# Key-value sums of the first pass as split products, with the pass's buffers laid out anew

## The chip, the cores and the metric

The kernel runs on one core of a Trainium2 chip. The metric is the device time of one launch in microseconds (us). Three runs of the kernel before took 457.25, 457.77 and 458.14 us, so the median is 457.77 us. Lower is better.

## The reference, cut to what matters

Four sequences of 2048 tokens with 256 features pass through a linear-attention block, a feed-forward block, a small iterative attention block that touches the first 16 tokens of every sequence, and the feed-forward block again. The change lies in the linear attention alone:

```python
x = _layernorm(x)                       # (4, 2048, 256)
q = elu(x @ Wq + bq) + 1                # 16 heads of 16 features
k = elu(x @ Wk + bk) + 1
v = x @ Wv + bv
kv = jnp.einsum('bkhd,bkhm->bhdm', k, v)      # sums over all tokens of a sequence
out = jnp.einsum('bqhd,bhdm->bqhm', q, kv) / max(q . sum(k), 1e-6)
```

The kernel doesn't form `v`. Since `v` is linear in the normalised tokens, it sums the 256 x 256 matrix G = kᵀ x over the tokens of a sequence, and multiplies G by Wv once per sequence. The last of the 256 columns of the normalised tokens is replaced by ones, which gives the sum of the keys for the normaliser. All of it is fp32. A product of fp32 accuracy is either one fp32 matmul, or several matmuls of type fp32r on a "high" part (the value rounded to fp32r) and a "low" part (what is left of it).

## The kernel before, in words

A *group* is 512 tokens: 4 tiles (`T = 4`) of 128 tokens. There are 16 groups (`NG`), 4 (`G`) to each of 4 sequences (`B`); n numbers the groups and g is n's place in its sequence. Pass 1 goes once over all groups, computing queries (kept in `q_all`) and G; pass 2 then goes over them again for everything else. Each engine has its own in-order program, the same loop `pass1(b, last)` on each of them, and they meet by semaphores only. The first sequence is unrolled, sequences 1 and 2 run in a hardware loop, the last is unrolled.

One group n of pass 1, engine by engine, in the order of each queue:

- TensorE (PE): `k_product(n)` is 24 fp32r matmuls of 256 columns into `PB` (L1212 to L1214); `q_product(n)` is 12 fp32r matmuls of 512 columns into `PA` (L1226 to L1228); `t1(n+1)` transposes the next group's normalised tokens into `PT` (L1168); `g_product(n)` is 8 fp32 matmuls of 256 columns into `PG` (L1236), each recorded as two. It waits for `k_done`.
- ScalarE (ACT): `ln1(n+1)` normalises the next group, 4 instructions (L535), after the statistics of group n+1 are in (`rstd1`) and after `g_product(n-1)`, which read the buffer of `xn` that is written; `exp_k` (L570) after `k_product(n)`; `exp_q` (L576) after `q_product(n)`; the high part `xt_hi` of the next group's transposes (L546, two).
- VectorE (DVE): the keys `k_tok` (L821) after `exp_k`; the layer-norm statistics of group n+2 (L740, L743); the low part `xt_lo` of the next group's transposes (L768, two) for which `k_product(n+1)` waits; the queries (L830).
- GpSimd (POOL): four small instructions that turn the statistics of a group into its scale and shift (L416 to L422; L418 is a power), and then `add_bo`, which adds a bias row to the tokens of the group before, 1024 elements a lane (L429).
- SyncE only loads tokens and weights.

At the first group of sequences 1 to 3, G of the sequence before is finished: DVE copies it to `g_sb` (L837), PE transposes it (L1244), ACT copies that (L583), PE multiplies by Wv (L1253, between the halves of `q_product`), and DVE masks the result into `kv_all` (L844, L848). Between the first and the second sequence DVE also prepares late weights: L784, L785, L787 and L855. All of them but L785 read two operands from SBUF.

`xn` has two buffers, `k_tok` one, and `exp_k` and `exp_q` share one.

Of the kernel before, what the change touches and what calls it, by code (L numbers as in the profile page):

```python
# [18 lines left out]
T = 4  # L19
# [25 lines left out]
def hybrid_kernel(nc, x_in, Wq, bq, Wk, bk, Wv, bv, Wo, bo, qw, qb, kw, vw, vb, ow, ob,  # L45
# [18 lines left out]
    with ExitStack() as ctx:  # L64
# [43 lines left out]
        SCR = 9 * 1024 + 8  # L108
        scratch = sb("scratch", [P, SCR])
        used = [0]  # L110

        def part(n):
            a = scratch[:, used[0]:used[0] + n]
            used[0] += n
            assert used[0] <= SCR
            return a

        xn = [part(T * D).rearrange("p (t d) -> p t d", t=T) for _ in range(2)]
# [4 lines left out]
        setup_start = used[0]  # L123
        wq_raw = part(C * D).rearrange("p (c n) -> p c n", c=C)
        wk_raw = part(C * D).rearrange("p (c n) -> p c n", c=C)
        bq_rows, bk_rows = part(D), part(D)
        minus_last, ident_less, to_last = [part(P) for _ in range(3)]
        used[0] = setup_start + 2 * C * GT
        wv, wo_raw = [part(C * D).rearrange("p (c n) -> p c n", c=C) for _ in range(2)]
        wv_last, bv_rows, bo_rows = [part(D) for _ in range(3)]  # L130
        g_sb = part(C * D).rearrange("p (c n) -> p c n", c=C)
        token_of = part(B * P)
        used[0] = 0
        o_tok = part(T * D).rearrange("p (k n) -> p k n", k=T * C)
        x2t = part(C * GT).rearrange("p (c n) -> p c n", c=C)
        h2, h2s, h3 = part(GT), part(GT), part(GT)
        y3 = part(T * D // 2).rearrange("p (t d) -> p t d", d=D)
        w1c = part(C * F).rearrange("p (c f) -> p c f", c=C)
# [4 lines left out]
        squares = o_tok.rearrange("p k n -> p (k n)").rearrange("p (c n) -> p c n", c=C)  # L143


        with ExitStack() as pass1_memory:
            def sb1(name, shape):
                return pass1_memory.enter_context(nc.sbuf_tensor(name, shape, F32R))

            wq_hi, wq_lo = sb1("wq_hi", [P, C, D]), sb1("wq_lo", [P, C, D])  # L150
            wk_hi, wk_lo = sb1("wk_hi", [P, C, D]), sb1("wk_lo", [P, C, D])
            xt_hi, xt_lo = sb1("xt_hi", [P, C, GT]), sb1("xt_lo", [P, C, GT])
# [8 lines left out]
        raw4 = [b_weights[:, 0, i, :].rearrange("p (c n) -> p c n", c=C) for i in range(4)]  # L161
        folded_all = b_weights[:, 1, :, :].rearrange("p i n -> p (i n)")
# [34 lines left out]
        after_raw = carve(b_weights[:, 0, :, :].rearrange("p i n -> p (i n)"))  # L197
# [16 lines left out]
        def one_batch_columns(wide):  # L214
# [25 lines left out]
        q_mm, q_exp, q_done = sem("q_mm"), sem("q_exp"), sem("q_done")  # L240
        g_mm, g_copied, gt_mm, gt_copied, kv_mm, kv_done = [
# [18 lines left out]
        (c_wts, c_vecs, c_xs, c_out, c_blk, c_bd, c_bd_sb, c_brow, c_brow_sb, c_fold, c_fold_sb, c_stat, c_rstd, c_z, c_zt, c_zt_sb,  # L260
         c_qkv, c_lin, c_k, c_vi, c_ss, c_rs, c_lt, c_q1, c_kn, c_knt, c_knm, c_vsel, c_vm, c_logit, c_lg, c_pr, c_pt, c_p1,
         c_inv, c_pv, c_o, c_ot, c_ot_sb, c_ql, c_dsum, c_diff, c_flag, c_proj, c_hid, c_relu, c_sq, c_ffn, c_added, c_final, c_zero,
         c_pool) = [sem(f"c_{n}") for n in (
             "wts", "vecs", "xs", "out", "blk", "bd", "bd_sb", "brow", "brow_sb", "fold", "fold_sb", "stat", "rstd", "z", "zt", "zt_sb",
             "qkv", "lin", "k", "vi", "ss", "rs", "lt", "q1", "kn", "knt", "knm", "vsel", "vm", "logit", "lg", "pr", "pt", "p1",
             "inv", "pv", "o", "ot", "ot_sb", "ql", "dsum", "diff", "flag", "proj", "hid", "relu", "sq", "ffn", "added", "final", "zero",
             "pool")]
# [41 lines left out]
        def _(sp):  # L309
# [69 lines left out]
            sp.wait_ge(c_final, 1)  # L379
# [10 lines left out]
        def _(pool):  # L390
# [45 lines left out]

            ln1(0)
            pool.wait_ge(norm1_dve, 2)
            ln1(1)
            pool.wait_ge(w2_loaded, 16 * 8)  # L440
            add_bo(0)
            with pool.Fori(2, NG) as n:
                ln1(n)
                add_bo(n - 1)
            add_bo(NG - 1)
# [84 lines left out]
        def _(act):  # L530
# [31 lines left out]
            def pass1(b, last):  # L562
                for g in range(G):
                    n = b * G + g
                    if not (last and g == G - 1):
                        ln1(n + 1, g + 1)

# [5 lines left out]
                    act.wait_ge(k_done, n + 1)  # L573

# [10 lines left out]
            act.wait_ge(setup_dve, 1)  # L585
            pass1(0, False)
# [140 lines left out]
        def _(dve):  # L727
# [84 lines left out]
            def pass1(b, last):  # L812
                for g in range(G):
# [122 lines left out]
            def step(g, b):  # L936
# [63 lines left out]
                if runs(r):  # L1000
# [4 lines left out]
                    if r == NG - 1:  # L1005
                        nc.vector.tensor_copy(dsum[0:SP, 7:8], x_s_out[:, 0:1]).then_inc(c_final, 1)
# [42 lines left out]
            def chain(i, slot):  # L1049
# [21 lines left out]
                elif at == (6, 1):  # L1071
                    dve.wait_ge(c_qkv, 1)
                    dve.wait_ge(c_brow_sb, 2)
                    nc.vector.tensor_tensor(kc.rearrange("p (c n) -> p c n", c=C), PG[0:SP, 0, D:2 * D].rearrange("p (c n) -> p c n", c=C),
                                            bias_k.rearrange("p (o n) -> p o n", o=1).to_broadcast([SP, C, P]), ALU.add).then_inc(c_k, 1)
                    nc.vector.tensor_tensor(lin, PG[0:SP, 0, 0:D], bias_q, ALU.add).then_inc(c_lin, 1)
                    nc.vector.tensor_tensor(vi, PG[0:SP, 1, 0:D], bias_v, ALU.add).then_inc(c_vi, 1)
                    dve.wait_ge(c_k, 1)
                    square_sums(kc, 0)
                elif at == (7, 1):  # L1080
                    dve.wait_ge(c_rs, 1)
                    link(nc.vector.tensor_tensor(heads(kc), heads(kc), over_feats(inv_std[0]), ALU.mult))
                    nc.vector.tensor_tensor(heads(kc), heads(kc), over_heads(l_w), ALU.mult).then_inc(c_kn, 1)
                    dve.wait_ge(c_vsel, 1)
# [3 lines left out]
                elif at == (7, 3):  # L1088
                    dve.wait_ge(c_knt, 1)
# [511 lines left out]
```

## Time and profile before

| | us |
|---|---|
| median of three runs | 457.77 |
| the profiled execution | 457.29 |
| its span, first to last instruction | 455.5 |
| TensorE busy | 425.2 (93%) |
| VectorE busy | 293.2 (64%) |
| ScalarE busy | 183.8 (40%) |
| GpSimd busy | 203.5 (45%) |
| granted TensorE clock, mean | 0.993 |

The time of the profiled execution is 1.8 us more than its span; it is 0.5 us below the median. Pass 1 takes the first 180 us of the span. Busy shares are means over the whole kernel, so they say which engine to look at, and the timelines of single engines within one group say what sets the pace there. In a timeline a row gives start, duration, engine, line, operation, and what it writes and reads; the duration of a TensorE row includes its pipeline, so the pace of matmuls is read from the chain of work, where a row's time is what it adds. Small GpSimd instructions are best read from start to start.

### The profile page before, as it was taken

Reading aid. Unit: us, or ns where it says so; the run is one execution under the profiler, and the core shown is the slowest. Engines: PE = TensorE matmul, PEld = TensorE weight load, DVE = VectorE, ACT = ScalarE, POOL = GpSimd, SP = SyncE. Lnnn points to the kernel's source line nnn. Section 1 sums busy time; section 2 is a strip of 40 time slices with the busy share of each in tenths; the row PEclk is TensorE's granted clock in tenths of the full one; section 3 lists DMA queues with packets and bytes.
Section 4 is the critical chain, followed back from the end, with each engine's and each line's share of the span. In section 5 each row is a group of like instructions: output and inputs, shape, how many; then the busy total and the mean of one; then the engine's idle time right before and its main releaser. Section 6 shows DMA issues by size and latency. Waiting matters only on the chain.

```text
span 455.5 us, 7618 instructions
## 1 busy us (share of the span) xinstructions
PE 425.2 (93%) x2570; PEld 354.7 (78%) x2570; DVE 293.2 (64%) x651; ACT 183.8 (40%) x321; POOL 203.5 (45%) x334
## 2 busy tenths in 40 slices
PE   7799989999999999688979999999999999999971
PEld 4689979998898999676858876878777787787851
DVE  4565575455556543459637697878858777887843
ACT  2464545555455541224134532333243323424440
POOL 3344442433334350036144367566527527635562
PEclk9999999999999999999999999999999999999997
DMA  8512111111100003100110111011010111011102
GB/s 260 179 48 78 63 47 46 48 46 46 46 0 1 0 2 89 8 2 3 51 46 4 50 49 35 15 48 47 4 47 1 50 48 35 16 49 47 48 32 71
DMA packets 22776, 20.58 MB, mean 45 GB/s; under 512 B 3255, under 2 KB 22717, under 8 KB 22717
## 3 DMA queue, kind: packets, MB, share of 16 engines
q1 hardware_dynamic: 22156, 19.32, 13.5%
q8 instruction: 30, 0.49, 0.4%
q10 hardware_dynamic: 560, 0.52, 0.4%
q14 instruction: 30, 0.24, 0.2%
HBM read 11.32 MB, written 8.45 MB: 43 GB/s over the span
## 4 chain that ended last, share of the span: by engine, by line
PE 82%; DVE 7%; ACT 5%; issue 2%; POOL 2%; DMA 1%; POOLq 0%; ACTq 0%; DVEq 0%
PE PG L1236 11%; PE PB L1356 6%; PE PT L1395 6%; PE PA L1356 5%; PE PB L1377 5%; PE PA L1425 4%; PE PA L1431 3%; PE PA L1426 3%; PE PA L1226 3%; PE PA L1227 3%; PE PA L1228 3%; PE PB L1214 3%; PE PB L1212 3%; PE PB L1213 3%; PE PT L1435 3%; PE PA L1367 3%
## 5 line engine op out<-in xcount | busy, mean ns | idle before, releaser
L454 POOL TENSOR_TENSOR ln_a<-ln_bn 128x4 f32<-128x4 f32 x32 | 6.5, 205 | 132.0 <-DVE ln_bn L934 132.0
L1236 PE MATMUL PG<-scratch 128*128 128x256 f32 x256 | 58.0, 379 | 1.3 <-DVE scratch L821 1.3
L821 DVE SCALAR_TENSOR_TENSOR scratch<-scratch,PB 128x1024 f32<-128x1024 f32 x16 | 19.5, 1221 | 60.3 <-ACT scratch L570 60.3
L1236 PEld LDWEIGHTS PG<-scratch 128*128 128x128 f32 x256 | 47.4, 190 | 7.4 <-issue 1.5
L535 ACT ACTIVATE scratch<-x_all,ln_shift,ln_rstd 128x255 f32 (+1 forms) x60 | 31.1, 589 | 36.7 <-PE PG L1236 30.2
L934 DVE BATCH_NORM_STATS2 ln_bn<-x_all 128x6 f32<-128x256 f32 x128 | 44.9, 413 | 0.9
L416 POOL TENSOR_SCALAR ln_rstd<-ln_mv 128x4 f32<-128x4 f32 x16 | 3.7, 228 | 91.3 <-DVE ln_mv L743 88.4
L1212 PE MATMUL PB<-wk_hi,xt_hi 128*128 128x256 f32 x128 | 39.0, 305 | 0.4 <-DVE xt_lo L768 0.4
L429 POOL TENSOR_TENSOR x_all<-x_all,scratch 128x1024 f32 (+1 forms) x16 | 38.2, 2388 | 0.6 <-ACT scratch L535 0.5
L429 POOL TENSOR_TENSOR x_all<-x_all,ob_rows 128x1024 f32<-128x1024 f32 x16 | 37.8, 2360 | 0.0
L695 ACT ACTIVATE scratch<-PA,ln_rsq 128x256 f32<-128x256 f32 x32 | 13.4, 471 | 59.3 <-PE PA L1356 35.4
L1425 PE MATMUL PA<-wo_hi,o_hi 128*128 128x256 f32 x128 | 33.5, 295 | 3.1 <-ACT o_hi L702 2.7
L1214 PE MATMUL PB<-wk_hi,xt_lo 128*128 128x256 f32 x128 | 36.2, 282 | 0.0
L1213 PE MATMUL PB<-wk_lo,xt_hi 128*128 128x256 f32 x128 | 36.1, 282 | 0.0
L463 POOL TENSOR_TENSOR ln_rsq<-ln_a,minus_ones 128x4 f32<-128x4 f32 x32 | 32.5, 1015 | 2.5
L1356 PE MATMUL PA<-ws,scratch 128*128 128x256 f32 x128 | 30.4, 380 | 2.7 <-ACT scratch L688 2.7
L990 DVE TENSOR_TENSOR x_all<-PA,x_all 128x1024 f32<-128x1024 f32 x16 | 19.6, 1225 | 20.6 <-PE PA L1431 20.6
L977 DVE TENSOR_TENSOR o_lo<-PB,o_hi 128x512 fp32r<-128x512 f32 x32 | 20.6, 684 | 18.6 <-ACT o_hi L702 18.5
L1426 PE MATMUL PA<-wo_lo,o_hi 128*128 128x256 f32 x128 | 31.9, 282 | 0.0
L1356 PE MATMUL PB<-ws,scratch 128*128 128x256 f32 x128 | 31.1, 386 | 0.0
L1395 PE MATMUL PT<-scratch 128*128 128x512 f32 x64 | 30.9, 605 | 0.0
L576 ACT ACTIVATE scratch<-PA,minus_one 128x1024 f32<-128x1024 f32 x16 | 17.8, 1115 | 30.2 <-PE PA L1228 28.9
(239 smaller groups left out, 1039.0 us busy)
## 6 DMA issues: line engine op xcount, KB each, us to landing
out_dram<-x_all SPq DMA_DIRECT2D x16, 512.0 KB, 3.1
x_all<-n_L_attn_a_inputs_q_dram SPq DMA_DIRECT2D x15, 512.0 KB, 3.6
x_all<-n_L_attn_a_inputs_q_dram ACTq DMA_DIRECT2D x2, 128.0 KB, 2.8
x_all<-n_L_attn_a_inputs_q_dram SPq DMA_DIRECT2D x2, 128.0 KB, 2.6
scratch<-in_L_attn_a_Wk_dram SPq DMA_DIRECT2D x1, 256.0 KB, 4.6
scratch<-in_L_attn_a_Wq_dram ACTq DMA_DIRECT2D x1, 256.0 KB, 5.0
scratch<-in_L_attn_a_Wv_dram SPq DMA_DIRECT2D x1, 256.0 KB, 6.8
scratch<-in_L_attn_a_Wo_dram SPq DMA_DIRECT2D x1, 256.0 KB, 6.2
```

The source lines that it names most:

```text
L429: nc.gpsimd.tensor_tensor(x_group(n), x_group(n), rows_[:, :].rearrange("p (o d) -> p o d", o=1).to_broadcast([P, T, D]), ALU.add).then_in ...
L463: nc.gpsimd.tensor_tensor(ln_rsq[:, slot, :], a, minus_ones[:, :], ALU.pow).then_inc(done, 1)
L535: nc.scalar.activation(dst[:, t:t + 1, 0:width], x_tile(n, t)[:, :, 0:width], ACT.Identity, scale=ln_rstd[:, slot, t:t + 1], bias=ln_shift ...
L934: nc.vector.bn_stats(ln_bn[:, slot, t:t + 1, :], x_tile(n, t)).then_inc(bn, 1)
L1212: mm(dst, hi, wk_hi[:, c, :], start=(c == 0), stop=False)
L1213: mm(dst, hi, wk_lo[:, c, :], start=False, stop=False)
L1214: last = mm(dst, lo, wk_hi[:, c, :], start=False, stop=(c == C - 1))
L1236: last = mm(PG[:, c, 0:D], k_tok[:, t, c * P:(c + 1) * P], xn[g % 2][:, t, :], start=(g == 0 and t == 0), stop=(g == G - 1 and t == T - 1))
L1356: last = mm(four(pair)[:, t, :], h[:, t * P:(t + 1) * P], ws2[:, :], start=True, stop=True)
L1395: last = mm(PT[:, 0, :], w1c[:, c, :], x2t[:, c, :], start=(c == 0), stop=(c == C - 1))
L1425: mm(four(PA)[:, t, :], hi, wo_hi[:, c, :], start=(c == 0), stop=False)
L1426: mm(four(PA)[:, t, :], hi, wo_lo[:, c, :], start=False, stop=False)
```

## The change

`g_product(n)` becomes two sets of fp32r matmuls. Keys are split into `k_hi` and `k_lo`, normalised tokens into the halves of `xn_pair`. The first set multiplies `k_hi` by both halves at once (8 matmuls of 512 columns, which fill a bank of `PG` with two sums), the second `k_lo` by the high half (8 of 256 columns). The high parts are copies by ACT (`x_high`, and the copy after `k_done`), `k_lo` is a subtraction by DVE ahead of `t1`, the low half of `xn_pair` a subtraction by POOL (`x_low`) behind `add_bo`. `ln1` on ACT now waits for `x_low` instead of `g_product`. The two sums of `PG` are added once a sequence by one more DVE instruction in `copy_g`.

`k_hi` and `k_lo` use the memory of `o_hi` and `o_lo`, which are idle in pass 1. The weights of set-up, of pass 1 and of pass 2 move to other places in SBUF, and the halves of `b_weights` swap. Eighteen single-use semaphores of the iterative attention become three counters (`c_once`, `c_made`, `c_taken`), with the same waits at the same places. Pass 2 issues the same instructions.

```diff
@@ POOL
+            def x_low(n, g):
+
+                ge_apart(pool, "pool", hi_done, 2 * n + 1)
+                nc.gpsimd.tensor_tensor(xn_pair[:, :, 1, :], xn[g % 2], xn_pair[:, :, 0, :].bitcast(F32), ALU.subtract).then_inc(x_lo, 1)
+
             ln1(0)
             pool.wait_ge(norm1_dve, 2)
             ln1(1)
+            x_low(0, 0)
             pool.wait_ge(w2_loaded, 16 * 8)
             add_bo(0)
-            with pool.Fori(2, NG) as n:
+            for n in range(2, G):
                 ln1(n)
                 add_bo(n - 1)
+                x_low(n - 1, n - 1)
...
@@ ACT
             def ln1(n, g):
-                ge_apart(act, "act", g_mm, n - 1)
+                ge_apart(act, "act", x_lo, n - 1)
                 normalise(xn[g % 2], n, 0, n, rstd1, norm1, D - 1)
+
+            def x_high(n, g):
+
+                ge_apart(act, "act", norm1, T * (n + 1))
+                ge_apart(act, "act", g_mm, n)
+                nc.scalar.activation(xn_pair[:, :, 0, :], xn[g % 2], ACT.Copy).then_inc(hi_done, 1)
...
                     if not (last and g == G - 1):
                         ln1(n + 1, g + 1)
+                    x_high(n, g)
 
                     act.wait_ge(k_mm, n + 1)
...
                     act.wait_ge(k_done, n + 1)
+                    nc.scalar.activation(k_hi, k_tok, ACT.Copy).then_inc(hi_done, 1)
 
                     ge_apart(act, "act", q_mm, C * (n + 1))
...
@@ DVE
                     if g == 0 and later_batch:
                         batch_kv(b - 1)
+                    dve.wait_ge(hi_done, 2 * n + 2)
+                    nc.vector.tensor_tensor(k_lo, k_tok, k_hi.bitcast(F32), ALU.subtract).then_inc(k_lo_done, 1)
                     if not (last and g == G - 1):
                         t1(n + 1, g + 1)
...
                 nc.vector.tensor_copy(g_sb[:, :, :], PG[:, :, 0:D]).then_inc(g_copied, 1)
+                dve.wait_ge(g_copied, 2 * b + 1)
+                nc.vector.tensor_tensor(g_sb[:, :, :], PG[:, :, D:2 * D], g_sb[:, :, :], ALU.add).then_inc(g_copied, 1)
@@ PE
-                pe.wait_ge(k_done, n + 1)
+                pe.wait_ge(hi_done, 2 * n + 2)
+                pe.wait_ge(x_lo, n + 1)
                 for t in range(T):
                     for c in range(C):
-                        last = mm(PG[:, c, 0:D], k_tok[:, t, c * P:(c + 1) * P], xn[g % 2][:, t, :],
-                                  start=(g == 0 and t == 0), stop=(g == G - 1 and t == T - 1))
+                        mm(PG[:, c, :], k_hi[:, t, c * P:(c + 1) * P], xn_pair[:, t, :, :].rearrange("p h d -> p (h d)"),
+                           start=(g == 0 and t == 0), stop=False, skip_group_check=True)
+                pe.wait_ge(k_lo_done, n + 1)
+                for t in range(T):
+                    for c in range(C):
+                        last = mm(PG[:, c, 0:D], k_lo[:, t, c * P:(c + 1) * P], xn_pair[:, t, 0, :],
+                                  start=False, stop=(g == G - 1 and t == T - 1), skip_group_check=True)
                 last.then_inc(g_mm, 1)
```

## Rows read from the trace of the kernel before

**Rows 1.** Page, part 4: shares of the chain of work that ended last.

```profile
PE 82%; DVE 7%; ACT 5%; issue 2%; POOL 2%; DMA 1%; POOLq 0%; ACTq 0%; DVEq 0%
```

**Rows 2.** Chain of work around group 9: start, time added, engine, tile, line.

```profile
112.95 0.12 PE PB L1214
113.07 0.23 PE PA L1226
...
115.82 0.87 PE PT L1168 x8
116.69 3.46 PE PG L1236 x16
```

**Rows 3.** Timeline of PE: the first matmul of `k_product` of groups 1, 3, 4, 5, 8, 9.

```profile
25.87 0.47 PE L1212 MATMUL PB<-wk_hi,xt_hi 128*128 128x256 f32 x1
...
45.76 0.47 PE L1212 MATMUL PB<-wk_hi,xt_hi 128*128 128x256 f32 x1
...
55.71 0.47 PE L1212 MATMUL PB<-wk_hi,xt_hi 128*128 128x256 f32 x1
...
68.57 0.47 PE L1212 MATMUL PB<-wk_hi,xt_hi 128*128 128x256 f32 x1
...
98.41 0.47 PE L1212 MATMUL PB<-wk_hi,xt_hi 128*128 128x256 f32 x1
...
109.85 0.47 PE L1212 MATMUL PB<-wk_hi,xt_hi 128*128 128x256 f32 x1
```

**Rows 4.** Timeline of DVE in group 9: keys, last of the statistics, low parts.

```profile
114.26 1.22 DVE L821 SCALAR_TENSOR_TENSOR scratch<-scratch,PB 128x1024 f32<-128x1024 f32 x1 [4.21 <-ACT scratch L570]
...
116.72 0.41 DVE L743 BATCH_NORM_AGGREGATE ln_mv<-ln_bn 128x2 f32<-128x6 f32 x4
117.58 1.29 DVE L768 TENSOR_TENSOR xt_lo<-PT,xt_hi 128x512 fp32r<-128x512 f32 x2 [0.45 <-ACT xt_hi L546]
```

**Rows 5.** Timeline of ACT in group 9.

```profile
110.55 2.08 ACT L535 ACTIVATE scratch<-x_all,ln_shift,ln_rstd 128x255 f32 x4 [2.47 <-PE PG L1236]
113.11 1.12 ACT L570 ACTIVATE scratch<-PB,minus_one 128x1024 f32<-128x1024 f32 x1 [0.48 <-PE PB L1214]
115.94 1.12 ACT L576 ACTIVATE scratch<-PA,minus_one 128x1024 f32<-128x1024 f32 x1 [1.72 <-PE PA L1228]
116.96 1.08 ACT L546 ACTIVATE xt_hi<-PT 128x512 fp32r<-128x512 f32 x2
```

**Rows 6.** Timeline of POOL in group 9: first statistics instruction, and `add_bo`.

```profile
117.40 0.23 POOL L416 TENSOR_SCALAR ln_rstd<-ln_mv 128x4 f32<-128x4 f32 x1 [7.02 <-DVE ln_mv L743]
...
119.47 2.39 POOL L429 TENSOR_TENSOR x_all<-x_all,scratch 128x1024 f32 x1
```

**Rows 7.** Timelines of ACT, DVE and POOL between the first two sequences.

```profile
53.79 0.64 ACT L588 ACTIVATE wo_hi<-scratch 128x512 fp32r<-128x512 f32 x1
...
55.86 2.42 DVE L784 TENSOR_TENSOR scratch<-scratch 128x512 f32<-128x512 f32 x1
...
58.92 0.68 DVE L855 TENSOR_TENSOR wo_lo<-scratch,wo_hi 128x512 fp32r<-128x512 f32 x1
...
55.32 2.41 POOL L429 TENSOR_TENSOR x_all<-x_all,scratch 128x1024 f32 x1
```

**Rows 8.** Groups of POOL by line, then DVE and POOL timelines where they overlap.

```profile
L461 POOL TENSOR_TENSOR ln_a<-ln_a,ln_d 128x4 f32<-128x4 f32 x32 | 6.7, 210 | 2.5
...
405.53 0.47 DVE L1138 SCALAR_TENSOR_TENSOR b_weights<-b_weights,q_all 64x256 f32<-64x256 f32 x1
...
405.61 0.45 POOL L461 TENSOR_TENSOR ln_a<-ln_a,ln_d 128x4 f32<-128x4 f32 x1
...
372.81 0.41 DVE L1095 TENSOR_TENSOR b_weights<-b_weights 64x256 f32<-64x256 f32 x1
...
372.71 1.02 POOL L463 TENSOR_TENSOR ln_rsq<-ln_a,minus_ones 128x4 f32<-128x4 f32 x1
```

**Rows 9.** Timeline of ACT in group 0: `exp_k`.

```profile
20.03 1.10 ACT L570 ACTIVATE scratch<-PB,minus_one 128x1024 f32<-128x1024 f32 x1
```

More of the change, by code:

```diff
@@ L105, in hybrid_kernel, with parts, take @@
         r_gap = sb("r_gap", [P, 4, T])
-        SCR = 9 * 1024 + 8
+        SCR = 4 * T * D
         scratch = sb("scratch", [P, SCR])
[L110 to L116, printed above, removed]
+        def parts(piece):
+            at = [0]
+            def take(n):
+                a = piece[:, at[0]:at[0] + n]
+                at[0] += n
+                assert at[0] <= piece.shape[1]
+                return a
+            return take
+        part = parts(scratch)
         xn = [part(T * D).rearrange("p (t d) -> p t d", t=T) for _ in range(2)]
@@ L122, in hybrid_kernel @@
         exp_q = exp_kq.rearrange("p (c n) -> p c n", c=C)
[L123 to L130, printed above, removed]
@@ L131, in hybrid_kernel @@
-        g_sb = part(C * D).rearrange("p (c n) -> p c n", c=C)
-        token_of = part(B * P)
-        used[0] = 0
+        k_hi, k_lo = [o[:, :, :].rearrange("p c n -> p (c n)").rearrange("p (t d) -> p t d", t=T) for o in (o_hi, o_lo)]
+        part = parts(scratch)
         o_tok = part(T * D).rearrange("p (k n) -> p k n", k=T * C)
         x2t = part(C * GT).rearrange("p (c n) -> p c n", c=C)
-        h2, h2s, h3 = part(GT), part(GT), part(GT)
+        h2, h3 = part(GT), part(GT)
         y3 = part(T * D // 2).rearrange("p (t d) -> p t d", d=D)
+        token_of = part(B * P)
@@ new lines, in hybrid_kernel, with sb1 @@
+        squares = o_tok.rearrange("p k n -> p (k n)").rearrange("p (c n) -> p c n", c=C)
+        with ExitStack() as pass1_memory:
+            def sb1(name, shape, dt=F32R, memory=pass1_memory):
+                return memory.enter_context(nc.sbuf_tensor(name, shape, dt))
+            with ExitStack() as setup_memory:
+                part = parts(sb1("setup", [P, T * 2 * D], F32, setup_memory))
+                wq_raw = part(C * D).rearrange("p (c n) -> p c n", c=C)
+                wk_raw = part(C * D).rearrange("p (c n) -> p c n", c=C)
+                bq_rows, bk_rows = part(D), part(D)
+                minus_last, ident_less, to_last = [part(P) for _ in range(3)]
+            xn_pair = sb1("xn_pair", [P, T, 2, D])
+            wq_hi, wq_lo = sb1("wq_hi", [P, C, D]), sb1("wq_lo", [P, C, D])
+            wk_hi, wk_lo = sb1("wk_hi", [P, C, D]), sb1("wk_lo", [P, C, D])
+            xt_hi, xt_lo = sb1("xt_hi", [P, C, GT]), sb1("xt_lo", [P, C, GT])
+            part = parts(sb1("wvo", [P, 9 * D], F32))
+            g_sb = part(C * D).rearrange("p (c n) -> p c n", c=C)
+            wv = part(C * D).rearrange("p (c n) -> p c n", c=C)
+            bo_rows = part(D)
+            wo_raw = part(C * D).rearrange("p (c n) -> p c n", c=C)
+            wv_last, bv_rows = part(D), part(D)
@@ L138, in hybrid_kernel @@
+        part = parts(sb("ffn_weights", [P, 5376 - GT])[:, :])
         w1c = part(C * F).rearrange("p (c f) -> p c f", c=C)
@@ L142, in hybrid_kernel @@
         ob_t = part(C * P).rearrange("p (c n) -> p c n", c=C)
[L143 to L152, printed above, removed]
+        h2s = sb("h2s", [P, GT])[:, :]
         b_weights = sb("b_weights", [P, 2, 4, C * D])
@@ L240, in hybrid_kernel @@
         q_mm, q_exp, q_done = sem("q_mm"), sem("q_exp"), sem("q_done")
+        hi_done, x_lo, k_lo_done = [sem(n) for n in ("hi_done", "x_lo", "k_lo_done")]
         g_mm, g_copied, gt_mm, gt_copied, kv_mm, kv_done = [
@@ L259, in hybrid_kernel @@
         c_link = sem("c_link")
[L260 to L267, printed above, removed]
+        c_wts, c_vecs, c_xs, c_out, c_blk, c_bd, c_brow, c_fold, c_fold_sb, c_stat = [sem(f"c_{n}") for n in (
+            "wts", "vecs", "xs", "out", "blk", "bd", "brow", "fold", "fold_sb", "stat")]
+        c_rstd, c_z, c_zt, c_zt_sb, c_lin, c_ss, c_rs, c_lt, c_q1, c_knm = [sem(f"c_{n}") for n in (
+            "rstd", "z", "zt", "zt_sb", "lin", "ss", "rs", "lt", "q1", "knm")]
+        c_vm, c_logit, c_lg, c_pr, c_pt, c_p1, c_inv, c_pv, c_o, c_ot = [sem(f"c_{n}") for n in (
+            "vm", "logit", "lg", "pr", "pt", "p1", "inv", "pv", "o", "ot")]
+        c_ot_sb, c_ql, c_zero, c_pool, c_once, c_made, c_taken = [sem(f"c_{n}") for n in (
+            "ot_sb", "ql", "zero", "pool", "once", "made", "taken")]
+        QKV, VSEL, KNT, DIFF, PROJ, HID, FFN = range(1, 8)
+        K, VI, KN, DSUM, FLAG, ADDED, FINAL = range(1, 8)
         waits_passed = {"sp": sem("sp_waits_passed"), "act": sem("act_waits_passed"),
@@ L439, in _ @@
             ln1(1)
+            x_low(0, 0)
             pool.wait_ge(w2_loaded, 16 * 8)
             add_bo(0)
-            with pool.Fori(2, NG) as n:
+            for n in range(2, G):
                 ln1(n)
                 add_bo(n - 1)
+                x_low(n - 1, n - 1)
+            with pool.Fori(1, B) as b:
+                for g in range(G):
+                    n = b * G + g
+                    ln1(n)
+                    add_bo(n - 1)
+                    x_low(n - 1, g + 1)
+            x_low(NG - 1, NG - 1)
             add_bo(NG - 1)
```

91 lines of the change are left out of this document (46 added, 45 removed).

## The prediction

> **What bounds the kernel now.** I read the chain of work first. It lies on TensorE for 82% [rows 1], and within pass 1 it is TensorE without a gap: in one group 24 steps of 0.12, 12 of 0.23, 0.87 for the transposes and 3.46 for the fp32 `g_product` [rows 2], in sum 9.97 us. The first matmuls of `k_product` confirm it: 9.95 us from group to group [rows 3]. Two kinds of group are longer: those that finish a sequence's G (11.44), and the one between the first and second sequence (12.86) [rows 3].
>
> Then I read the other engines' timelines within a group, because a shorter `g_product` only helps as far as they keep up. I count from e, the start of `exp_k` [rows 5]. DVE makes the keys from e+1.15 to e+2.37 and its statistics end at e+4.02 [rows 4]. POOL starts on them at e+4.29 and is done at e+6.35, where `add_bo` takes over until e+8.75 [rows 6]. ACT and DVE pass on the next transposes by e+5.8 [rows 4, 5]. So one circuit of `exp_k`, keys, transposes, next `k_product` has about 1 us of slack in 9.95, not more. The reader is to see that TensorE is the bound, with a circuit through the other three engines close behind.
>
> The third thing is how DVE and POOL disturb each other. L784, a DVE subtraction of 512 elements with two SBUF operands, took 2.42 us where L855 of the same size took 0.68; it began during `add_bo`, which ended at 57.73, and itself ended 0.55 us later [rows 7]. The reverse also shows: POOL's L461, 0.21 us in the mean of 32, took 0.45 when it began during DVE's L1138 (two SBUF operands), and ended 0.06 us after it [rows 8]. Instructions with an operand in PSUM run beside POOL unstretched: the low parts at 117.58 keep their 1.29 next to L416 [rows 4, 6]. The change adds one such instruction per group on each of the two engines.
>
> **The change part by part.**
>
> *TensorE.* Removed: 3.46 us a group. Added: 8 matmuls of 512 columns at 0.23 and 8 of 256 at 0.12 [rows 2], in sum 2.80. If nothing else bound, a group would take 9.3 us, and 16 groups would save 10.5.
>
> *ACT.* `x_high` and the `k_hi` copy, 1024 elements each from SBUF. The trace has none of that size; 1024 from PSUM take 1.12 [rows 5], and 512 from SBUF take 0.64 [rows 7]. Bounds are 1.12 and twice 0.64, 1.28. I take 1.16, near the lower, since one instruction has one overhead, and let the next instruction start after 1.06 (the two PSUM ones start 1.02 apart). Nothing hides them fully, since both stand ahead of something that is waited for: `x_high` ahead of `exp_k`, `k_hi` ahead of `exp_q` and of `g_product`.
>
> *Circuit A, through the keys.* From e: keys e+2.37, `k_hi` e+3.56, `exp_q` starts e+3.46, the two transposed high parts end by e+5.6. On DVE `k_lo` runs from e+4.0 to e+5.2 (twice L855's 0.68 less one overhead: 1.21, [rows 7]), and the low parts then end at e+6.4. `g_product` starts at e+3.6 and ends at e+6.5. `k_product(n+1)` starts about e+6.45, takes 2.9 and some 0.25 for its first matmul. So circuit A is 9.6 us, and the new TensorE time of 9.3 isn't reached: TensorE waits 0.3 us a group.
>
> *Circuit B, through the statistics.* `ln1(n+1)` on ACT stands ahead of `x_high(n)` and `exp_k(n)`, and it needs POOL's scale of group n+1, which comes from statistics made after the keys of n-1. From e of n-1: POOL done e+6.35, `ln1` until e+8.4, `x_high` until e+9.4, then `exp_k(n)`: 9.5 us, if POOL isn't held up. But `k_lo` holds DVE's two SBUF reads from e+4.0 to e+5.2, and L416 wants to begin at e+4.29. By rows 8 it ends about 0.06 after `k_lo`, 0.7 us later than now, with no more than 0.13 of it absorbed. Circuit B is then 10.1 us, longer than A, and longer than the 9.95 of now.
>
> *x_low.* 1024 elements on POOL, 2.39 by `add_bo` [rows 6], bounds 1.2 (DVE's L821 has as many elements, [rows 4]) to 3.5 (half as much again for the strided fp32r output, which no row shows). It starts at e+0.15 and ends at e+2.5, ahead of `g_product` at e+3.6 with 1 us to spare, and away from `k_lo`. In a normal group it costs nothing; at 3.5 it still ends in time.
>
> *Groups that finish a sequence.* There the statistics are made long before `k_lo`, which waits for L844, so the collision is nearly gone; POOL's power instruction (L463's kind) let DVE's L1095 run in its 0.41 [rows 8], so I don't let L418 block. TensorE saves its 0.65, and `ln1`'s delay carried over from the group before takes back 0.35: 11.15 for 11.44. The group after it takes 9.6. The addition in `copy_g`, 0.68 as L855 [rows 7], ends before `k_product` does: nothing.
>
> *Start.* `exp_k(0)` starts at 20.03 and `k_product(1)` at 25.87 [rows 3, 9]. Now `x_high(0)` stands ahead: `exp_k(0)` at 21.1, keys until 23.5, `k_hi` until 24.6. On POOL `x_low(0)` (21.2 to 23.6) pushes `add_bo(0)` to between 23.6 and 26.0. `k_lo(0)` is ready at 25.1, is blocked until 26.0 and ends at 27.2; the second low part ends at 28.4. `k_product(1)` starts at 28.45: +2.6. L416 follows `k_lo(0)`, POOL is done at 29.1, and `ln1(2)` and `x_high(1)` put `exp_k(1)` at 32.1. The next three groups are 10.1 each: +0.45. So `k_product(4)` starts at 58.75 and `exp_k(4)` at 62.4.
>
> *Between the first two sequences.* Before, L784 waited for `add_bo` [rows 7], and the rest fitted. Now POOL has `add_bo(4)` from 59.3 to 61.7 and, as soon as `x_high(4)` ends at 62.5, `x_low(4)`. L784 ends 0.55 after `add_bo(4)`, at 62.25; L785 follows; L787 is ready at 62.5, a draw with `x_low(4)`. If it loses, it waits until 64.95 and takes 0.47 (L1138's time, [rows 8]), and L855 ends at 66.1; if it wins, L855 loses the next draw and ends at about the same time. Before, L855 ended at 59.6, and `k_product` of the next group started 8.97 later [rows 3, 7]. Now TensorE saves 0.65 of that and the addition in `copy_g` puts 0.68 on it: 75.05. The group takes 16.3 for 12.86: +3.45.
>
> *Rest.* In the last group nothing covers the `k_hi` copy: `exp_k(15)` comes 3.2 after the start of `k_product(15)`, and 3.56 and 2.8 later `g_product` ends. That is 9.6, against 9.4 by the same count with keys at 2.37 and `g_product` at 3.46, or +0.2 (at least 0, as `g_product(15)` can't start sooner than TensorE is free; at most 0.9, all of the exposed copy). Behind it the added `copy_g` instruction is hidden: TensorE has the first products of pass 2 ahead of the transposes of G. Uncovered it would cost its 0.68. Pass 2 issues the same work; new places in SBUF and shared counters: 0, as no wait is added. Set-up: 0.
>
> Sum, new less old: start +2.6; groups 1 to 3 +0.45; between sequences +3.45; sequence 1 (9.6, 10.1, 10.1 against three of 9.95) -0.05; sequence 2 (11.15, 9.6, 10.1, 10.1) -0.35; sequence 3 (11.15, 9.6, 10.1) -0.5; last +0.2. That is +5.8 on the profiled 457.29: 463.1, taken as 463.0. The profiled execution lies 0.5 under the median of the three runs, inside the rounding of this sum.
>
> **The rivals.**
>
> *POOL isn't delayed by `k_lo`.* L461 is a single case, and L1138 has 64 lanes. Then circuit B is 9.5 and A sets the pace: 0.46 less in 7 groups, 0.3 in 2, 0.5 at the boundary: -4.3, so 458.7.
>
> *Faster: operations with an fp32r output stay off the shared resource.* Every stretched DVE row writes plain fp32, and L855, the one with fp32r output, met no POOL instruction [rows 7]. Its place is wherever `k_lo`, L855 and `x_low` meet the other engine, its price what the sum charges there: the 4.3 above, 1.0 at the start, 2.4 where L787 would not wait for `x_low(4)`. It decides once circuit A (9.6) is the longest in most groups. 463.0 - 7.7 = 455.3. Against it: the reads are as in L784.
>
> *`x_low` is dear.* At 3.5 us it lengthens the start and the blocked L787 by 1.1 each: 465.2; and if two of the late-weight instructions are blocked instead of one, 467.6.
>
> *The power instruction blocks too.* By the row it doesn't. The Trainium skill ("SBUF — State Buffer", section on the two separate sides) says that the pair of ports shared by DVE and GpSimd is locked for the whole instruction and the loser fully blocks, for a DVE operation with two SBUF inputs as well. It agrees with L784 and L461; for L1095, which ran in 0.41 inside a power instruction, the trace disagrees. As a mechanism here: `k_lo` is blocked by L418 in the two groups that finish a sequence and behind the boundary, 0.7 each: 465.1.
>
> **How the numbers follow.** Forecast 0.50 (own range 461 to 465.5); POOL not delayed 0.14; faster 0.12; dear `x_low` 0.14; power blocks 0.06; the rest mishaps on either side. A measurement can tell about 0.2%, 0.9 us. Slower by more: 0.50 + 0.14 + 0.06 and half of POOL not delayed, with some of the rest, 0.79; same 0.09; faster 0.12. The range is 458.0 to 467.0; it takes in all but the faster case and the far end.
>
> **What would show each step.** Starts of `k_product` 10.1 apart in most groups, 9.6 in one after each G: circuit B. L416 ending just after `k_lo`: the blocking. L787 or L855 near 2.7 us: the boundary. `k_product(1)` at 28.4: the start. `k_product` starts 9.6 apart throughout mean that POOL runs on; 9.3 that both circuits are mis-sized. The prediction is wrong above all if `k_lo` and L416 don't meet.

## The result, and the profile after

The changed kernel takes 466.12 us in the median (465.63 to 467.02), against 457.95 us for the kernel before measured beside it: a ratio of 1.018, with a 95% interval of 1.015 to 1.0205. It is 8.2 us slower. The forecast was 463.0 us, in a range of 458.0 to 467.0.

The profiled execution of the changed kernel took 466.44 us. First the page: its span, and the shares of the chain of work that ended last.

```profile
span 464.7 us, 7704 instructions
...
PE 57%; DVE 14%; ACT 13%; issue 7%; POOL 5%; DVEq 1%; DMA 1%; POOLq 1%; ACTq 0%
```

The chain was 82% TensorE before [rows 1]. Now a quarter of it lies on VectorE and ScalarE: TensorE has less to do in pass 1 and no longer sets the pace there. The first matmuls of `k_product`, the counterpart of [rows 3], for groups 1, 3, 4, 6, 7 and 8:

```profile
29.56 0.36 PE L1257 MATMUL PB<-wk_hi,xt_hi 128*128 128x256 f32 x1
...
49.03 0.36 PE L1257 MATMUL PB<-wk_hi,xt_hi 128*128 128x256 f32 x1
...
59.02 0.36 PE L1257 MATMUL PB<-wk_hi,xt_hi 128*128 128x256 f32 x1
...
87.41 0.34 PE L1257 MATMUL PB<-wk_hi,xt_hi 128*128 128x256 f32 x1
...
97.57 0.34 PE L1257 MATMUL PB<-wk_hi,xt_hi 128*128 128x256 f32 x1
...
107.72 0.33 PE L1257 MATMUL PB<-wk_hi,xt_hi 128*128 128x256 f32 x1
```

Normal groups are 10.15 us apart, where it was 9.95. The same starts for all groups, read from the timelines of both kernels, give the whole account of the 9.2 us between the spans:

| stretch | before | after | difference | forecast |
|---|---|---|---|---|
| until `k_product(1)` starts | 25.87 | 29.56 | +3.7 | +2.6 |
| groups 1 to 3 | 29.84 | 29.46 | -0.4 | +0.45 |
| group 4, between the first two sequences | 12.86 | 18.89 | +6.0 | +3.45 |
| rest of sequence 1 | 29.84 | 29.81 | 0.0 | -0.05 |
| sequence 2 | 41.28 | 41.39 | +0.1 | -0.35 |
| sequence 3 without its last group | 31.34 | 30.78 | -0.55 | -0.5 |
| last group, to the end of `g_product(15)` | 9.42 | 9.76 | +0.35 | +0.2 |
| pass 2 and end of the span | 275.05 | 275.05 | 0.0 | 0 |

So the loss is at two places, and the other fourteen groups together come out 0.5 us shorter. One normal group, on ScalarE, VectorE and GpSimd (the counterparts of [rows 4 to 6]; L609 is `exp_k`, L578 `x_high`, L868 `k_lo`, L458 `x_low`, L434 the first statistics instruction, L447 `add_bo`):

```profile
88.23 2.08 ACT L567 ACTIVATE scratch<-x_all,ln_shift,ln_rstd 128x255 f32 x4 [1.80 <-POOL ln_shift L440]
90.21 1.04 ACT L578 ACTIVATE xn_pair<-scratch 128x1024 fp32r<-128x1024 f32 x1
91.16 1.10 ACT L609 ACTIVATE scratch<-PB,minus_one 128x1024 f32<-128x1024 f32 x1
93.54 1.06 ACT L613 ACTIVATE o_hi<-scratch 128x1024 fp32r<-128x1024 f32 x1 [1.29 <-DVE scratch L862]
```

```profile
94.74 0.41 DVE L784 BATCH_NORM_AGGREGATE ln_mv<-ln_bn 128x2 f32<-128x6 f32 x4
95.07 1.19 DVE L868 TENSOR_TENSOR o_lo<-scratch,o_hi 128x1024 fp32r<-128x1024 f32 x1
96.18 1.28 DVE L809 TENSOR_TENSOR xt_lo<-PT,xt_hi 128x512 fp32r<-128x512 f32 x2
```

```profile
91.43 2.41 POOL L458 TENSOR_TENSOR xn_pair<-scratch,xn_pair 128x1024 fp32r<-128x1024 f32 x1 [1.01 <-ACT xn_pair L578]
95.43 0.92 POOL L434 TENSOR_SCALAR ln_rstd<-ln_mv 128x4 f32<-128x4 f32 x1 [1.59 <-DVE ln_mv L784]
```

L434 begins while `k_lo` runs and takes 0.92 instead of 0.23 [rows 6]; it ends 0.09 after `k_lo`. And ScalarE's three instructions follow each other without a gap behind a wait of 1.80 for GpSimd: `exp_k` is issued as soon as the queue lets it, not when `k_product` is done. That is circuit B of the forecast, as drawn.

### The profile page after: what moved, and what is told of

It reads as the page before. It is cut to its first block, busy times and chain, and to the rows that moved or that the text cites. A ratio compares the mean times of both kernels' runs of the same rounds, so it can differ in the third digit from the quotient of the medians.

```text
span 464.7 us, 7704 instructions
## 1 busy us (share of the span) xinstructions
PE 423.5 (91%) x2570; PEld 349.5 (75%) x2570; DVE 317.9 (68%) x671; ACT 213.2 (46%) x353; POOL 251.1 (54%) x350
## 4 chain that ended last, share of the span: by engine, by line
PE 57%; DVE 14%; ACT 13%; issue 7%; POOL 5%; DVEq 1%; DMA 1%; POOLq 1%; ACTq 0%
PE PB L1407 6%; PE PA L1407 5%; PE PT L1446 5%; PE PB L1428 5%; PE PA L1476 4%; ACT scratch L609 3%; PE PA L1482 3%; PE PA L1477 3%; ACT scratch L567 3%; PE PG L1282 3%; PE PT L1486 3%; PE PA L1418 2%; DVE ln_bn L781 2%; ACT o_hi L743 2%; ACT xn_pair L578 2%
## 5 line engine op out<-in xcount | busy, mean ns | idle before, releaser
L458 POOL TENSOR_TENSOR xn_pair<-scratch,xn_pair 128x1024 fp32r<-128x1024 f32 x16 | 38.4, 2400 | 25.2 <-ACT xn_pair L578 25.2
L1282 PE MATMUL PG<-xn_pair,o_hi 128*128 128x512 f32 x128 | 35.6, 422 | 8.0 <-ACT o_hi L613 7.1
L447 POOL TENSOR_TENSOR x_all<-x_all,wvo 128x1024 f32 (+1 forms) x16 | 38.5, 2404 | 0.1
L447 POOL TENSOR_TENSOR x_all<-x_all,ob_rows 128x1024 f32<-128x1024 f32 x16 | 37.7, 2358 | 0.0
L1257 PE MATMUL PB<-wk_hi,xt_hi 128*128 128x256 f32 x128 | 37.1, 290 | 0.4 <-DVE xt_lo L809 0.4
L1282 PEld LDWEIGHTS PG<-xn_pair,o_hi 128*128 128x128 f32 x128 | 23.9, 196 | 15.9 <-ACT o_hi L613 6.6
L434 POOL TENSOR_SCALAR ln_rstd<-ln_mv 128x4 f32<-128x4 f32 x16 | 11.9, 746 | 39.3 <-DVE ln_mv L784 36.2
L755 ACT ACTIVATE scratch<-PT,w1ob 128x512 f32<-128x512 f32 x16 | 11.0, 688 | 46.4 <-PE PT L1486 46.4
L1407 PE MATMUL PB<-ws,h2s 128*128 128x256 f32 x128 | 31.1, 386 | 0.0
```

Of the source, the lines that this page charges most:

```text
L447: nc.gpsimd.tensor_tensor(x_group(n), x_group(n), rows_[:, :].rearrange("p (o d) -> p o d", o=1).to_broadcast([P, T, D]), ALU.add).then_in ...
L458: nc.gpsimd.tensor_tensor(xn_pair[:, :, 1, :], xn[g % 2], xn_pair[:, :, 0, :].bitcast(F32), ALU.subtract).then_inc(x_lo, 1)
L1257: mm(dst, hi, wk_hi[:, c, :], start=(c == 0), stop=False)
L1282: mm(PG[:, c, :], k_hi[:, t, c * P:(c + 1) * P], xn_pair[:, t, :, :].rearrange("p h d -> p (h d)"), start=(g == 0 and t == 0), stop=False, ...
L1407: last = mm(four(pair)[:, t, :], h[:, t * P:(t + 1) * P], ws2[:, :], start=True, stop=True)
```

## The experiments

**Keeping TensorE busy in its long waits.** The two places that cost more than forecast have something in common that I had not charged. At the start and in group 4:

```profile
24.31 3.75 PE L1282 MATMUL PG<-xn_pair,o_hi 128*128 128x512 f32 x8 [3.25 <-ACT o_hi L613]
...
67.39 1.12 PE L1295 MATMUL PG<-ident,wvo 128*128 128x128 f32 x4 [5.26 <-DVE wvo L882]
...
69.16 0.63 PE L1273 MATMUL PA<-xt_hi,wq_lo 128*128 128x512 f32 x1
69.59 0.63 PE L1271 MATMUL PA<-xt_hi,wq_hi 128*128 128x512 f32 x1
```

Eight matmuls of 512 columns take 3.75 us behind a wait of 3.25, where a normal group has 2.13; and behind the wait of 5.26 in group 4 they follow 0.43 apart instead of 0.23. The mean granted clock of these stretches (the figure before DMA's share) fits:

```profile
core 0: us, PE busy (x) PEld busy (x) DVE busy (x) ACT busy (x) POOL busy (x), PEclk, DMA share, GB/s
...
24.00:36.00 12.00, 11.69 (x59) 10.40 (x60) 7.16 (x15) 7.22 (x11) 8.93 (x7) 0.76 0.14 46
...
60.00:80.00 20.00, 13.82 (x84) 12.23 (x84) 16.27 (x24) 10.49 (x16) 9.07 (x8) 0.91 0.09 27
```

It was 1.00 in these stretches of the kernel before. A mean of 0.76 is a part of the stretch at 1.2 GHz and the rest at 2.4: read in steps of half a microsecond, the clock is 0.50 from 22.9 to 29.7 us and from 67.3 to 70.7. It falls 1.8 us into the first wait, and at the end of the second. Does it matter, or does the slow work lie beside other waits?

```diff
+                    if True and n == G:
+                        for _ in range(6):
+                            mm(PT[:, 0, :], ones_f[:, :], g_t[:, :, :].rearrange("p c n -> p (c n)"), start=True, stop=True)
                     if later_batch:
                         g_transposes(b - 1)
...
+                    if True and n == 0:
+                        for _ in range(3):
+                            mm(PG[:, 0, :], ones_f[:, :], g_t[:, :, :].rearrange("p c n -> p (c n)"), start=True, stop=True)
                     g_product(n, g)
 
-            pass1(0, False)
-            with pe.Fori(1, B - 1) as b:
+            for b in range(B - 1):
                 pass1(b, False)
```

The last lines are a second edit: TensorE's program for sequences 1 and 2 is written out instead of looped, here and in every kernel below that has the extra matmuls. What it is worth by itself shows in the kernels further down: with it `g_product` starts 0.79 us after the start of the transposes in groups 4 and 8, without it 0.95, so some 0.16 us in each of these two groups.

> The changed kernel with TensorE kept busy in its two long waits of pass 1: three extra fp32 matmuls of 512 columns before g_product of group 0, six before the transposes of G in group 4 (their results are overwritten). Theory (the waits let the granted clock fall, and the matmuls behind them run at half pace): the matmuls of 512 columns behind the waits return from 0.43 to 0.23 us, k_product(1) starts about 1 us earlier, and group 4 lasts 16.3 to 17 us instead of 18.9, since L893 then comes before add_bo and isn't blocked; in sum 3 to 4 us less than the changed kernel, about 462.5. Rival (the excess over the forecast is all blocking of L893 and k_lo by GpSimd, and the slow matmuls lie beside it): within 1 us of the changed kernel's 466.1, and L893 still takes over 2 us.

Measured: 462.67 us, 1.011 of the kernel before (1.0077 to 1.0143), 3.45 less than the changed kernel. More work on TensorE made the kernel faster; by these two groups, some 0.3 us of the 3.45 is the written-out loop. Group 4 took 16.20, where the forecast without a falling clock had said 16.3, and group 4's start came 1.2 earlier. The trace has the full pace, and L893 unblocked:

```profile
24.23 2.13 PE L1282 MATMUL PG<-xn_pair,o_hi 128*128 128x512 f32 x8 [0.62 <-ACT o_hi L613]
...
67.36 0.40 PE L1271 MATMUL PA<-xt_hi,wq_hi 128*128 128x512 f32 x1
67.60 0.39 PE L1272 MATMUL PA<-xt_lo,wq_hi 128*128 128x512 f32 x1
...
69.47 0.22 DVE L893 TENSOR_SCALAR kv_all<-head_mask,wvo 128x8 f32 x1
```

In the changed kernel the second L893 was this:

```profile
72.53 2.24 DVE L893 TENSOR_SCALAR kv_all<-head_mask,wvo 128x8 f32 x1
...
72.38 2.37 POOL L447 TENSOR_TENSOR x_all<-x_all,wvo 128x1024 f32 x1
```

So the slow matmuls delayed the product with Wv by 1.5 us, which let VectorE's masking fall into `add_bo`, which held it for 2 more. TensorE's `g_product(4)` waits for the masking itself, because the masking still reads the sums in `PG`:

```profile
75.02 2.11 PE L1282 MATMUL PG<-xn_pair,o_hi 128*128 128x512 f32 x8 [0.92 <-DVE kv_all L893]
```

Of the 2.7 us that group 4 lost, 1.5 are the slow pace ahead of this wait, and the wait and the looped start of `g_product` are the rest. The two costs aren't separate: the wait is a consequence of the slow pace.

**`k_lo` with an operand in PSUM.** The same instruction in the same place, with one SBUF operand.

```diff
-nc.vector.tensor_tensor(k_lo, k_tok, k_hi.bitcast(F32), ALU.subtract)
+nc.vector.tensor_tensor(k_lo, four(PB), k_hi.bitcast(F32), ALU.subtract)
```

> The changed kernel, with the subtraction that makes k_lo reading the key sums in PSUM instead of k_tok in SBUF: the same length and place in the queue, but one SBUF operand instead of two (so k_lo isn't the low part of the keys). Theory (two SBUF operands keep GpSimd's first statistics instruction out): L434 takes 0.23 us instead of 0.97, the groups follow each other in 9.5 to 9.6 us instead of 10.15, about 3.5 to 4.5 us less in all, 461.5 to 462.5. Rival (the subtraction costs by its time on VectorE alone, or 10.15 comes from elsewhere on the path): spacing stays above 10.0 and the time within 1 us of 466.1.

Measured: 461.53 us, 1.0071 (1.0041 to 1.01). The groups follow each other in 9.55 to 9.6. VectorE's instruction is as long as ever, and GpSimd's is not held:

```profile
103.24 1.19 DVE L868 TENSOR_TENSOR o_lo<-PB,o_hi 128x1024 fp32r<-128x1024 f32 x1
...
103.55 0.23 POOL L434 TENSOR_SCALAR ln_rstd<-ln_mv 128x4 f32<-128x4 f32 x1 [1.64 <-DVE ln_mv L784]
```

The length of `k_lo` on VectorE therefore costs nothing beyond circuit A; what costs 0.55 to 0.6 us a group is that its two SBUF operands keep GpSimd out. The saving of 4.6 us is just above what was expected (0.55 to 0.6 in the normal groups, 0.5 in the two that finish a sequence).

**Late weights spread over groups 0 to 2.** One or two behind the queries of each of these groups, instead of four in a row in front of group 4: the counterpart of L784 behind group 0, of L785 and L787 behind group 1, of L855 behind group 2. ScalarE's copy of `wo_hi` moves to group 0. Cut to what matters:

```diff
+                    if isinstance(b, int) and b == 0:
+                        late_weights(n)
...
             pass1(0, False)
-            dve.wait_ge(w2_loaded, 16 * 8)
-            take_last_row(wv, wv_last, bv_rows, wv_row, 0.0)
-            dve.wait_ge(w_split, 3)
-            nc.vector.tensor_tensor(wo_lo[:, :, :], wo_raw, wo_hi[:, :, :].bitcast(F32), ALU.subtract).then_inc(setup_dve, 1)
```

> The changed kernel, with the four late-weight instructions of VectorE (and the copy of wo_hi on ScalarE) spread over groups 0 to 2, one or two behind the queries of each, instead of all between groups 3 and 4. Theory (they are blocked by add_bo and x_low in turn and all of it is on the path): group 4 takes about 11.3 instead of 18.9 with no clock dip in it, groups 0 to 2 lose at most 1 us together, 459 to 460 in all. Rival (the blocking moves with them into groups 0 to 2): the time stays above 463.

Measured: 459.2 us, 1.0025 (1.0008 to 1.0042): 6.9 us less than the changed kernel. Group 4 took 11.59, and groups 1 to 3 9.51, 9.89 and 9.96, no longer than in the changed kernel. `k_product(1)` came 15.56 after `k_product(0)` instead of 16.61; the half clock lasted 3.4 us there (25.7 to 29.1) instead of 6.8, so this 1.05 isn't shown to be the edit's. The instructions are still blocked, and it costs nothing where VectorE has to wait for `exp_k` anyway:

```profile
30.76 2.47 DVE L828 TENSOR_TENSOR wvo<-wvo 128x512 f32<-128x512 f32 x1
34.55 1.22 DVE L876 SCALAR_TENSOR_TENSOR scratch<-scratch,PB 128x1024 f32<-128x1024 f32 x1 [1.32 <-ACT scratch L609]
```

**`x_high` ahead of `ln1`.** Circuit B goes through `ln1`, `x_high` and `exp_k` in ScalarE's queue. `x_high` doesn't need the statistics, so it can use the time in which ScalarE waits for them.

```diff
+                    x_high(n, g)
                     if not (last and g == G - 1):
                         ln1(n + 1, g + 1)
-                    x_high(n, g)
```

> The changed kernel, with x_high(n) issued ahead of ln1(n+1) on ScalarE instead of behind it, where it fills ScalarE's wait for the statistics. Theory (the circuit through statistics, ln1, x_high and exp_k sets 10.15 in most groups): exp_k no longer stands behind both, the spacing falls to the other circuit's 9.6 to 9.7, 3 to 4 us less, 462 to 463. Rival (the circuit through keys and transposes, or TensorE's waits, sets the pace already): spacing stays at 10.1 and the time within 1 us of 466.1.

Measured: 461.12 us, 1.0073 (1.0048 to 1.0099), 5.0 less than the changed kernel. The spacing is 9.6 in normal groups, though L434 is blocked as before:

```profile
95.61 1.06 ACT L578 ACTIVATE xn_pair<-scratch 128x1024 fp32r<-128x1024 f32 x1 [1.25 <-PE PG L1287]
96.58 2.06 ACT L567 ACTIVATE scratch<-x_all,ln_shift,ln_rstd 128x255 f32 x4
98.55 1.10 ACT L609 ACTIVATE scratch<-PB,minus_one 128x1024 f32<-128x1024 f32 x1
...
102.77 0.97 POOL L434 TENSOR_SCALAR ln_rstd<-ln_mv 128x4 f32<-128x4 f32 x1 [2.02 <-DVE ln_mv L784]
```

This and the PSUM operand take away different links of the same circuit, and both arrive near 9.6. What takes over isn't quite the same. Circuit A alone, where `exp_k` waits for `k_product`, is 9.5: `exp_k` then starts 3.08 us after `k_product` does. Here it starts 3.19 to 3.22 after, in every group from 1 to 14, and never waits for TensorE itself: `x_high` needs the buffer that `g_product` reads, and waits for its end (1.25 in the first row), and `ln1` and `exp_k` follow without a gap. That is a third circuit, `g_product`, `x_high`, `ln1`, `exp_k`, keys, `k_hi`, 0.1 us longer than A. The edit gave more than expected (5.0 against 3 to 4), and 1.9 us lie at the start, where `k_product(1)` comes 14.7 after `k_product(0)` instead of 16.6: `exp_k(0)` starts 1.0 sooner, and the half clock is 3.4 us long (24.3 to 27.7) instead of 6.8.

**All of it together.** Late weights spread, `x_high` first, and `add_bo(0)` ahead of `x_low(0)` on GpSimd, so that it doesn't meet `k_lo(0)`. The edits are those above and this one:

```diff
             ln1(1)
-            x_low(0, 0)
             pool.wait_ge(w2_loaded, 16 * 8)
             add_bo(0)
+            x_low(0, 0)
```

> The changed kernel with three edits at once: late weights spread over groups 0 to 2, x_high(n) ahead of ln1(n+1) on ScalarE, and add_bo(0) ahead of x_low(0) on GpSimd (which was idle there), so that k_lo(0) isn't blocked. Theory (three separate causes, each at its own place): spacing 9.6 in normal groups, 11.0 in the three that finish a sequence, group 4 among them, and 1 us less at the start; the first to the last k_product is then 152 to 153 us apart, where the kernel before has 157.9, and the time is 452 to 453.5. Rival (the gains overlap, since removing one lets another wait take its place): 456 to 458, no better than the kernel before.

Measured: 455.36 us, 0.9936 of the kernel before (0.9915 to 0.9957). It is faster than the kernel before, but by 2.6 us and not by the 5 that I expected. From the first to the last `k_product` it took 154.6, not 152 to 153. Two things were missed: `k_product(1)` came no earlier than with `x_high` first alone (14.76 after `k_product(0)`, against 14.73), and group 2 took 10.73. The profiled execution, 456.99, is 1.6 over the median; two more stretches of 3.4 us at half clock lie in it, in set-up and in pass 2, outside the groups compared here. The next two runs are about these.

> As the combined kernel, and in addition the three extra fp32 matmuls in TensorE's wait before g_product of group 0. Theory (the granted clock falls there in the combined kernel too): 0.5 to 1.2 us less than the combined kernel. Rival (with k_lo(0) unblocked the slow matmuls lie beside other work): no difference beyond 0.3 us.

Measured with the three extra matmuls: 453.11 us, 0.990 (0.9878 to 0.9921). That is 2.2 less, more than expected. `k_product(1)` comes 13.26 after `k_product(0)`, 1.5 less, and groups 4 and 8 take 10.89 and 10.90 instead of 11.06 and 11.07, which is the written-out loop. In the combined kernel `g_product(0)` had again run slowly behind a wait of 2.30, and the unblocked `k_lo(0)` had gained nothing:

```profile
24.75 3.40 PE L1294 MATMUL PG<-xn_pair,o_hi 128*128 128x512 f32 x8 [2.30 <-ACT o_hi L613]
```

Group 2 still took 10.73. With `x_high` issued earlier, `x_low` follows `add_bo` at once, and of two late-weight instructions each meets one of them:

```profile
36.88 2.03 DVE L830 TENSOR_SCALAR wvo<-wvo 128x256 f32<-128x256 f32 x1
38.95 2.50 DVE L832 SCALAR_TENSOR_TENSOR wvo<-wvo,ident 128x256 f32<-128x256 f32 x1
41.37 1.21 DVE L876 SCALAR_TENSOR_TENSOR scratch<-scratch,PB 128x1024 f32<-128x1024 f32 x1
```

L830 adds 0.0 to a bias row, so it can go, and each group has one instruction:

```diff
-                    nc.vector.tensor_scalar(bv_rows, bv_rows, 0.0, None, ALU.add).then_inc(wv_row, 1)
-                    dve.wait_ge(wv_row, 2)
-                    nc.vector.scalar_tensor_tensor(wv[:, 1, :], ...).then_inc(wv_row, 1)
+                    dve.wait_ge(wv_row, 1)
+                    nc.vector.scalar_tensor_tensor(wv[:, 1, :], ...).then_inc(wv_row, 2)
```

> The combined kernel with the extra matmuls, but with no more than one late-weight instruction behind the queries of a group: the one that adds 0.0 to the bias row is dropped, as it changes nothing. In the combined kernel group 2 took 10.73 instead of 9.6, since that instruction was blocked by add_bo and the one behind it (L832, 2.50 us) by x_low. Theory (a single blocked instruction ends before the next keys are due, a second doesn't): group 2 takes 9.6, 1.0 to 1.1 us less, about 452.1, the fastest kernel of this study. Rival (the one that is left is blocked by x_low all the same): group 2 stays at 10.7 and the time at 453.1.

Measured: group 2 takes 9.60, and the remaining instruction, blocked once (2.16), ends before `exp_k`. The time is 453.06 us, 0.9893 (0.9866 to 0.992). The microsecond is in the trace, whose span of 449.4 is 1.5 under that of the run before; in the medians of two separate comparisons, whose executions spread over 1.8 and 3.3 us, it doesn't show. These two kernels are the fastest of the study, some 1% ahead of the kernel before.

**What the split product is worth.** Part of that lead is the spread of the late weights, which has nothing to do with the product. So the kernel before with that edit alone:

> The kernel before, with only its late-weight instructions spread over groups 0 to 2 in the same way. Theory: group 4 falls from 12.86 to about 11.45 us, the other groups stay at 9.95 since TensorE bounds them, 1.2 to 1.5 us less, about 456.4; the combined kernel is still 3 to 4 us ahead of it, which is what the split product itself then gives. Rival (the blocked instructions hold up groups 0 to 2 here too): within 0.5 us of the kernel before.

Measured: 456.45 us, 0.9967 (0.9952 to 0.9982). Group 4 fell from 12.86 to 11.45 and all other groups stayed at 9.95 to 11.45. Against this the last kernel is 3.4 us ahead, with `x_high` first, `add_bo(0)` first, the extra matmuls with the written-out loop, and one instruction dropped: 0.35 us in a normal group, 0.55 in one that finishes a sequence, with 0.6 given back at the start. Between the first and the last `k_product` the two traces are 4.9 apart. The cheaper matmuls had promised 10.5.

## Why the prediction was right, and where it was short

The direction and its reason were right. *TensorE gains 0.65 a group that it can't use*: confirmed. Where nothing holds it, its parts start 2.88 (`k_product`), 2.75, 0.79 and 2.87 (`g_product`) apart, in sum 9.3 as forecast, against 3.06, 2.75, 0.87 and 3.27 before. But in each normal group of every kernel with the split, `g_product` starts about 0.05 after the `k_hi` copy ends (group 9 below). *Circuit A, 9.6*: confirmed, a little long. The groups behind each finished sequence of the changed kernel show it alone, at 9.5, and with one operand in PSUM it is 9.55; the 9.60 to 9.63 of the kernels with `x_high` first are the third circuit described above, which the forecast didn't have. *Circuit B, 10.1, because `k_lo` holds back L434*: confirmed at 10.15, with the blocking and the spacing both removed by a change of operand; the rival in which GpSimd isn't delayed is out. That an operand in PSUM avoids the blocking rested on rows that overlap L416 by 0.05 us only [rows 4, 6]; the run with that operand shows it, with 0.23 inside 1.19. *`x_low` harmless in a normal group, 2.39*: 2.41, harmless. The rival of a dear `x_low` is out, and with it the one in which fp32r outputs avoid the conflict: `k_lo` has such an output and blocks, and at the start it was blocked in turn (2.07 for 1.19).

```profile
124.78 1.06 ACT L613 ACTIVATE o_hi<-scratch 128x1024 fp32r<-128x1024 f32 x1 [1.29 <-DVE scratch L862]
...
125.89 2.13 PE L1282 MATMUL PG<-xn_pair,o_hi 128*128 128x512 f32 x8
```

The power instruction: the Trainium skill ("SBUF — State Buffer", section on the two separate sides) has the loser of the shared ports block for the whole of the other's instruction. Here the trace disagrees again, now in pass 1: in group 8 `k_lo` began 0.07 after L436 did, ran beside it for 0.98, and took its usual 1.22, as L436 took its usual 1.05.

```profile
116.11 1.22 DVE L868 TENSOR_TENSOR o_lo<-scratch,o_hi 128x1024 fp32r<-128x1024 f32 x1
...
116.04 1.05 POOL L436 TENSOR_TENSOR ln_rstd<-ln_rstd,minus_half 128x4 f32<-128x4 f32 x1
```

Three terms were mis-sized. The sum was 5.8 and the spans differ by 9.2.

- *Start*, forecast +2.6, measured +3.7. The chain up to `k_lo(0)` was right (blocked by `add_bo(0)`, end at 26.7 against a forecast 27.2). Missing was the pace of `g_product(0)` after TensorE's wait. With TensorE kept busy, `k_product(1)` starts at 27.94. Groups 1 to 3 then gave most of it back: `exp_k(1)` had its own date by circuit B (forecast 32.1, measured 32.70), and `k_product(4)` came at 59.02 against a forecast 58.75.
- *Between the sequences*, forecast +3.45, measured +6.0. The draw between the late weights and `x_low(4)` went as described: the instruction at L828 won it (0.48), the one at L900 lost and took 2.83, and the transposes of G began at 67.39, as by the forecast's count. What came behind was costed at the pace of the kernel before, 7.65 us: it took 10.5, by the lower clock and by the masking that it pushed into `add_bo`. Kept busy, the group took 16.20, so that these two are nearly the whole of the missing 2.6.
- *Groups that finish a sequence*, forecast 11.15, measured 11.57 and 11.31. `g_product` isn't the cause: from its start to the next `k_product` it took 2.85 and 2.87, against 2.80 forecast. The delay of `ln1` carried over from the group before was put at 0.35 and is 0.6 and 0.5: `exp_k` stands ahead of the copy of the transposed G on ScalarE, and the product with Wv waits 0.47 and 0.35 for that copy. With circuit B removed by the PSUM operand, these groups took 11.02 and 10.84. Group 8 has 0.16 of TensorE's loop on top.

The step of the forecast that fell short is thus mainly one, behind the first two terms, whose excess is 3.7 us: the sum took every TensorE duration from rows in which TensorE never waits for long, and used them behind waits of 3 and 5 us that follow from the forecast's own times. The total stayed within the stated range in part by luck: the rivals that gave the range its upper part, a dear `x_low` and a power instruction that blocks, didn't come.

## What to carry to other kernels

Before an engine's work is made shorter, write down the other circuits that close once per turn of the loop, each with the queue order it depends on. The gain ends at the longest of them, and an instruction placed ahead of a waited-for one belongs to the circuit, however idle its engine is on average. A change of queue order closes new circuits: write them down again. Where VectorE and GpSimd both work on SBUF, cost each pair that can meet, and put work without a deadline where its engine waits anyway, one instruction at a time. If a change makes TensorE wait as long as here, 2.3 us and more, cost what follows at the lower clock as well.

## What was not expected of the hardware

- Behind waits of 2.30, 3.25 and 5.26 us, matmuls ran at half pace (0.43 for 0.23 us at 512 columns) until 3.8, 5.4 and 3.3 us after the wait's end, at a granted clock of 0.50. Filling the waits with matmuls nobody needs, and writing TensorE's loop out, made the kernels 3.45 and 2.2 us faster; by their traces the loop's part is 0.3. With the waits filled the clock stood at 1.00 throughout pass 1. In the kernel before, the longest such wait in pass 1 was under 1.4 us, and the clock stood at 1.00.
- An instruction of VectorE with one tensor in SBUF and a scalar is blocked by GpSimd as well: L893, 128x8, took 2.24 us instead of 0.22, and L830, 128x256, took 2.03 instead of 0.28. The forecast had counted on instructions with two SBUF operands only.
- 1024 elements on ScalarE from SBUF took 1.04 to 1.06, less than the 1.10 to 1.12 from PSUM, where I had estimated 1.16. The first are copies and the second exponentials, so the runs don't say which of the two makes the difference.
